# Recurrence with a mixture-of-experts layer: TensorE's up products three tiles ahead, VectorE's routing steps spread, scales of the sorted tiles on GpSimd, x and outputs in pairs of tiles

## The reference

```
h[t] = tanh(x[t] @ Wx + b + h[t-1] @ Wh)            # per batch element
shared  = silu(h @ w1_shared.T) @ w2_shared.T       # hidden width 1024
logits  = h @ gate_w.T                              # 8 experts
top 2 experts of each token, gates = softmax of the two logits
out = x + shared + sum over the token's 2 experts of gate * (silu(h @ w1_e.T) @ w2_e.T)
```

## Time and profile before

| | us |
|---|---|
| median of three runs | 382.14 |
| lowest, highest | 379.4, 389.73 |
| the profiled execution | 384.39 |
| its span | 382.6 |
| TensorE, ScalarE, VectorE, GpSimd busy | 357.1, 239.3, 197.2, 103.4 |
| mean granted TensorE clock, share of full speed | 0.985 |

### The profile page before, as it was taken

One profiled execution on the slowest core, in us unless ns is written; L12 is line 12 of the kernel. 1 busy time (PEld: TensorE's weight loads), 2 busy tenths in 40 slices (PEclk: granted clock), 3 DMA queues, 4 the chain that ended last, 5 costly groups with the idle time before them and its releaser, 6 DMA issues.

```text
span 382.6 us, 8882 instructions
## 1 busy us (share of the span) xinstructions
PE 357.1 (93%) x2440; PEld 252.5 (66%) x2441; DVE 197.2 (52%) x421; ACT 239.3 (63%) x462; POOL 103.4 (27%) x99
## 2 busy tenths in 40 slices
PE   7979999988897799899999999999999999999991
PEld 6758899954664465565666666666666666666670
DVE  0599999977999784574432333332333323233310
ACT  2877888875965675583566565666555666555630
POOL 1000001000027888220032522333322333322342
PEclk9999999999999699999999999999999999999997
DMA  7999999408699999698999898888888888888982
GB/s 222 430 428 433 422 398 334 147 17 134 153 177 230 229 265 223 175 210 172 193 155 135 158 165 145 161 153 153 152 148 144 159 152 153 151 150 144 160 138 29
DMA packets 167322, 75.55 MB, mean 197 GB/s; under 512 B 149504, under 2 KB 163968, under 8 KB 166016
## 3 DMA queue, kind: packets, MB, share of 16 engines
q1 hardware_dynamic: 155408, 61.93, 66.4%
q0 software_dynamic: 6864, 9.11, 15.8%
q10 hardware_dynamic: 5024, 4.20, 4.0%
HBM read 23.68 MB, written 16.53 MB: 105 GB/s over the span
## 4 chain that ended last, share of the span: by engine, by line
PE 73%; DMA 7%; SPq 6%; issue 5%; ACT 3%; another core or an unknown queue 2%; DVE 1%; POOL 1%; POOLq 0%; ACTq 0%
PE py L1170 28%; PE z L1062 27%; PE z L1078 8%; PE z L1043 4%; SPq L352 3%; PE z L1011 2%; SPq L378 2%; DMA space<-x_cols 2%; DMA space<-space 1%; DMA sorted_rows<-space 1%; PE px L1054 1%; ACT space L912 1%; PE py L1011 1%; DMA out<-space 1%
## 5 line engine op out<-in xcount | busy, mean ns | idle before, releaser
L1170 PE MATMUL py<-w_slots,space 128*128 (+1 forms) x1272 | 149.7, 274 | 7.0 <-DMA space<-recurrence_w 3.1
L1062 PE MATMUL z<-w_slots,x 128*128 (+1 forms) x636 | 148.4, 382 | 5.0 <-issue 4.1
L1170 PEld LDWEIGHTS py<-w_slots,space 128*128 128x128 f16 x1272 | 124.6, 98 | 35.5 <-issue 7.6
L1062 PEld LDWEIGHTS z<-w_slots,x 128*128 128x128 f16 x636 | 62.2, 98 | 71.8 <-issue 9.7
L912 ACT ACTIVATE space<-z,tile_scales 128x512 f32<-128x512 f32 x106 | 71.8, 677 | 50.6 <-PE z L1062 41.7
L488 POOL DMA_INDIRECT out<-space x37 | 58.2, 1574 | 153.2 <-issue 56.3
L637 DVE SCALAR_TENSOR_TENSOR recurrence_w<-space,tile_scales,recurrence_w 128x512 f16<-128x512 f32 x54 | 40.3, 751 | 75.8 <-ACT recurrence_w L919 64.8
L637 DVE SCALAR_TENSOR_TENSOR space<-space,tile_scales 128x512 f16<-128x512 f32 x52 | 38.7, 750 | 62.6 <-ACT space L919 53.4
L581 DVE SCALAR_TENSOR_TENSOR w_slots<-w_slots,w_scale 128x1024 f16<-128x1024 f32 x36 | 46.2, 1285 | 1.0
L919 ACT ACTIVATE recurrence_w<-space,tile_scales 128x512 f16<-128x512 f32 x54 | 39.0, 722 | 9.9 <-ACT space L912 3.1
L919 ACT ACTIVATE space<-space,tile_scales 128x512 f16<-128x512 f32 x52 | 37.5, 722 | 7.7 <-ACT space L912 2.7
(11 more groups left out here) (121 smaller groups left out, 162.5 us busy)
## 6 DMA issues: line engine op xcount, KB each, us to landing
w_slots<-weights SPq DMA_DIRECT2D x8, 2048.0 KB, 30.4
sorted_rows<-pad_row SPq DMA_DIRECT2D x1, 5070.0 KB, 57.7
w_slots<-weights SPq DMA_DIRECT2D x2, 1024.0 KB, 10.4
space<-x_rows ACTq DMA_DIRECT2D x16, 128.0 KB
out<-space ACTq DMA_DIRECT2D x16, 128.0 KB
space<-x_cols SPq DMA_DIRECT2D x3, 512.0 KB, 9.7
space<-recurrence_w SPq DMA_TRANSPOSE x55, 2.4
space<-space SPq DMA_TRANSPOSE x52
```

Of the source, the lines that this page charges most:

```text
L1062: last = nc.tensor.matmul(Z[u % 2][h][:], x16[:, u, x_part, k], weight(f, k * HID + h * BANK, BANK, part), start=k == 0 and x_part == 0 an ...
L1170: last = nc.tensor.matmul(PY[p][:, 0:D], hiddenT[:, p, low, q], weight(f, MATRIX + q * D, D, part), start=q == 0 and not low and part == 0 ...
```

## The change

It touches the shared stage and what prepares the sorted one.

- TensorE does the up products of tiles 2 and 3 before the down product of tile 0 and stays three tiles ahead (`LEAD`). The loop holds tiles 1 to 12; the down product of tile 13 follows alone. In this stage `up` waits for each half of `Z` by itself. `Z`, `PY` and the turned copies keep two buffers each.
- ScalarE takes the silu of tile 0's first half before it waits for the branch on `drift_known`. The code of the branch not taken is shorter, and one `If` on TensorE is two.
- VectorE: `states_low`, the halves of tiles 0 and 1 and the routing steps are interleaved; `route_gates` is after `route_choice`, `route_slots` at g = 2, `route_rows` at g = 3, the last `find_scales` at g = 6, `route_tiles` at g = 10; `shared_y(g - 3)` comes ahead of the side work; weight splits start at g = 4 instead of 3.
- The scales of the sorted tiles are made by GpSimd after its last scatter, with 12 instructions instead of VectorE's 6; the reduction of the last bounds comes after the first tile's scatters. ScalarE's first `high` no longer waits for `tiles_ok` but for `scales_ok`, at g = 7.
- SyncE: six row buffers instead of eight; one row transpose ahead of each part of tile 0's turn instead of three behind; other tables. The first two pairs of x are loaded in the recurrence. Later loads and the stores move two tiles in one DMA each.

```diff
-SORT_RING = 8
+SORT_RING = 6
+LEAD = 3
+PAIRS = TILES // 2
-ROWS_AT = {0: (0, 1, 2), 1: (3,), 3: (4, 5), 4: (6, 7), 5: (8, 9), **{t - 4: (t,) for t in range(10, TILES)}}
+ROWS_AT = {1: (2,), 2: (3, 4), 3: (5,), 4: (6,), 5: (7, 8), 6: (9, 10), 7: (11,), 8: (12, 13), 9: (14,), 10: (15,)}
...
+            sp.wait_ge(xproj_mm, K * BLOCKS)
+            for j in range(2):
+                sp.dma_start(x_res[:, 2 * j:2 * j + 2], x_pairs[j]).then_inc(x_res_in[j], 16)
...
             def turn_row(t):
                 sp.wait_ge(x_lo_ok, t + 1)
-                if t == RING:
-                    sp.wait_ge(routed, 1)
                 if t >= SORT_RING:
-                    sp.wait_ge(sorted_ok[t % SORT_RING], 16 * TOP)
+                    sp.wait_ge(sorted_ok[t % SORT_RING], 16 * TOP * (t // SORT_RING))
...
+            turn_first()
+            turn_row(0)
+            turn_part(0, 0, 0)
+            turn_row(1)
+            turn_part(0, 0, 1)
...
+            def make_scales():
+                def step(instruction):
+                    steps[0] += 1
+                    instruction.then_inc(table_step, 1)
+                    pool.wait_ge(table_step, steps[0])
+                steps = [0]
+                pool.wait_ge(experts_ok, 1)
+                pool.wait_ge(scales_ok, 1)
+                for n in range(3):
+                    step(nc.gpsimd.tensor_mul(scale_parts, is_expert,
+                                              ffn_scales[:, n, 1:FFNS].unsqueeze(1).broadcast_to([P, SLOT_TILES, E])))
+                    for half in (E // 2, E // 4):
+                        step(nc.gpsimd.tensor_add(scale_parts[:, :, 0:half], scale_parts[:, :, 0:half], scale_parts[:, :, half:2 * half]))
+                    step(nc.gpsimd.tensor_add(tile_scales[:, TILES:ALL_TILES, n], scale_parts[:, :, 0], scale_parts[:, :, 1]))
+                pool.sem_inc(tiles_ok, 1)
...
+                if t == 0:
+                    reduce_bounds(len(BOUND_BATCHES) - 1)
+                v = t - SORT_RING // 2
+                if 0 <= v < TILES - SORT_RING:
+                    waited(sorted_ok[v % SORT_RING], 16 * TOP * (v // SORT_RING + 1))
+                    nc.gpsimd.tensor_copy(hr[:, v % SORT_RING, D:ROW], meta[:, v + SORT_RING]).then_inc(row_copied, 1)
+            make_scales()
...
+            act.wait_ge(split_ok, 1)
+            act.wait_ge(up_mm, 1)
+            silu_first(hidden_ok)
             act.wait_ge(drift_known, 1)
...
+            def store(j):
+                v = j % 2
+                act.wait_ge(y_ok, 2 * j + 2)
+                nc.scalar.dma_start(out_pairs[j], ys[:, 2 * v:2 * v + 2]).then_inc(stored[v], 16)
+                if j + 2 < PAIRS:
+                    nc.scalar.dma_start(x_res[:, 2 * v:2 * v + 2], x_pairs[j + 2]).then_inc(x_res_in[v], 16)
...
-                if not (isinstance(g, int) and g < AHEAD):
-                    pe.wait_ge(hidden_ok, (g - 1) * HALVES)
                 for h in range(HALVES):
+                    if arrived is None:
+                        pe.wait_ge(hidden_ok, g * HALVES - (2 * HALVES - h - 1))
+                    elif h == 0:
+                        pe.wait_ge(hidden_ok, (g - 1) * HALVES)
                     up_half(u, f, h, up_mm)
...
             def shared(g, u, n):
-                up(g + AHEAD, (u + AHEAD) % RING, SHARED)
+                up(g + LEAD, (u + LEAD) % RING, SHARED)
                 down(g, u % 2, n, SHARED)
-            for g in range(2):
-                shared(g, g, 16 * (g // 2 + 1))
-            with pe.Fori(0, TILES // RING - 1) as i:
-                for u in range(2, 2 + RING):
+            up(AHEAD, AHEAD, SHARED)
+            shared(0, 0, 16)
+            with pe.Fori(0, (TILES - RING) // RING) as i:
+                for u in range(1, 1 + RING):
                     shared(i * RING + u, u, i * 32 + 16 * (u // 2 + 1))
+            down(TILES - LEAD, (TILES - LEAD) % 2, 16 * ((TILES - LEAD) // 2 + 1), SHARED)
```

More of the change, by code:

```diff
@@ L964, in _ @@
                     nc.scalar.mul(high, whole, scale).then_inc(high_ok, 1)
-                if g > AHEAD:
-                    store(g - AHEAD - 1)
+                if g >= LEAD + 2 and g % 2:
+                    store((g - LEAD - 2) // 2)
+            act.wait_ge(tiles_ok, 1)
             def expert(t, u, n, outs, indexed):
@@ L1124, in _ @@
                 pe.wait_ge(up_mm, 2 * HALVES)
+                pe.wait_ge(hidden_ok, 1)
                 with pe.Fori(0, GENERAL_ROUNDS) as r:
-                    inject_first()
                     pe.wait_ge(start_ok_general, r + 1)
-                    round_(z_mm_general, h_ok_general, r)
+                    for i in range(2):
+                        general_pair(r, i, i, first=i == 0)
+                    with pe.Fori(1, L // 4) as j:
+                        for p in range(2):
+                            general_pair(r, j * 2 + p, p)
+            with pe.If(same != EXPECTED_SAME):
                 for k in range(K):
```

191 lines of the change are left out of this document (100 added, 91 removed).

## The result

The changed kernel took 388.31 us in the median of four runs (387.0 to 389.3), the kernel before 381.11 us beside it (379.4 to 389.73). The ratio is 1.020, with a 95% interval of 1.014 to 1.026. I had forecast 375 us, 368 at the least and 382 at the most; it became slower, by an amount that lies on the 2% mark. The profiled execution of after took 387.0 us with a span of 385.3 us.

The account below looks back on a forecast made before the run. TensorE's products bound the sorted stage, so time could only come from some 15 us lost before it; 3.2 (start) + 1.3 (later wait) + 2.9 (slow matmuls) = 7.4 us off 382.14 gave 375 us, range 368 to 382.

Parts of the forecast that it names:

- Scales on GpSimd: Behind the last scatter: twelve GpSimd steps take 10.3 us, `tiles_ok` at 165.1 us; cost 0, bounds 0 and 3.7 us.
- the sum: Whole kernel: 3.2 + 1.3 + 2.9 = 7.4 us gained, taken off both the profiled execution and the median of 382.14 us.
- my slower rival: Before the sorted tiles: late last scatter and 1.24 us steps put `tiles_ok` at 180.7 us; 389 us, chance 0.07.
- Routing and sorting: Ahead of the sorted tiles: scatters begin sooner, last issued by 154.8 us, up product possible at 163.4 us; costs nothing.
- 2.6 us of cover: At the first sorted up product: sorted rows allow it at 163.4 us, below the 166.05 us at which TensorE gets there.
- Three tiles ahead: Start of the shared stage: the longer lead of up products removes 3.2 us of TensorE's waits, bounds 0.6 and 3.9.
- the 1.63, 0.78 and 0.76 us: Start of the shared stage: TensorE's waits for turned parts and VectorE's output of tile 0, all claimed to go.
- the 0.77 us that I had kept: Start of the shared stage: TensorE's wait for ScalarE's silu, claimed to stay because the branch behind stays.
- a rival (0.23): Shared stage: six row buffers and SyncE's queue turn all but the start's 3.2 us into waits; 379 us, chance 0.23.
- the next step: Later in the shared stage: the 1.30 us wait for tile 5's turned part goes; 0 if SyncE waits for scatters.
- Gaps of the trips: Up product 8 and the third trip's start: idle parts of 1.67 + 1.75 and 2.99 us claimed to stay.
- the slow part of 2.9 us: Behind the gaps in up product 8: matmuls slowed at the lower clock, claimed to go, 2.9 us, bounds 0 and 2.9.

Follow-up runs that it names:

- run 1: Changed kernel with the sorted tiles' scales back on VectorE, all else as changed: 379.6 us, ratio 1.004 to the kernel before.
- run 4: Changed kernel with one 128x4 copy more on GpSimd, behind the last scatter and ahead of the scales: 387.65 us in one execution.
- run 6: The kernel before, unchanged, measured and profiled a second time: 384.96 us, span 383.3 us.
- run 5: Kernel before with only the sorted tiles' scales moved to GpSimd behind the last scatter: 394.6 us in one execution, beside 382.9 us for before.
- run 8: Kernel before with 96 router instructions more in a branch never taken, so TensorE's shared-tile loop stands further on: 391.38 us, before 386.61 us, no verdict.
- run 11: Kernel before with only the up products three tiles ahead instead of two, shared outputs moved to match: 387.78 us, before 381.74 us, no ratio.
- run 12: Changed kernel with scales on VectorE and up products two tiles ahead again, outputs behind the routing steps: 385.58 us, ratio 1.013 to before.
- run 13: Changed kernel with scales on VectorE and row transposes 6 to 15 one or two places later on SyncE: 383.25 us, ratio 1.005 to before.
- run 14: Changed kernel with scales on VectorE and row transposes 6 to 15 each one place later on SyncE: 382.06 us, ratio 1.005 to before.
- run 15: Changed kernel with scales on VectorE and its two routing steps there moved sooner: 384.78 us, ratio 1.010 to before.
- run 16: Changed kernel with scales on VectorE, routing steps sooner, and the row transposes as in run 14: 383.51 us, ratio 1.007 to before.
- run 2: Changed kernel with one 128x4 sum more on GpSimd, ahead of its wait for the routing: 393.6 us in one execution.
- run 3: Changed kernel with one 128x4 sum more on GpSimd, between the scatters of tiles 12 and 13: 385.37 us in one execution.
- run 10: Kernel before with TensorE's loop over the shared tiles written out, nothing else: 382.48 us, ratio 1.010 to before.

## Why the prediction was wrong

Two steps of the prediction failed: the scales on GpSimd, which I put at a cost of 0, and the sum, whose 7.4 us did not come off the median. On the chip of run 1 the parts can be told apart. The kernel before took 378.02 us there; my forecast, 375/382.14 of it, would have been 371.0. Run 1 took 379.6, 8.6 us more, and run 4 with the scales on GpSimd 387.65, another 8.1 us. Of the 8.6 us, run 1's profile names 5.9 at down product 6 (4.25 of waiting and 4.46 - 2.78 = 1.7 of slow matmuls), for which my sum had no term; how the rest divides is not shown.

**Scales on GpSimd: the first step that failed.** I bounded twelve instructions by the durations of a VectorE product and of GpSimd's longest copy, and the busy time was inside the bounds: 6.6 us. What I left out is the gap that GpSimd takes to change from reductions to products, 8.38 us here, 5.9 to 8.4 us in every run that changed kinds. The last reduction across partitions stands at 109.69 us and the products behind the last scatter, so the gap falls on the path. `tiles_ok` came at 173.7 instead of 165.1 us. That is the threshold of my slower rival, 173.45 us, and about its result (389 us, at a chance of 0.07), but by another road: its steps of 1.24 us and its last scatter at 165.8 us were both wrong. And the price could be read. In the kernel before, GpSimd's timeline begins so:

```profile
1.23 0.32 POOL L423 MEMSET pad_row<- 128x260 f32 x1
9.18 0.28 POOL L425 TENSOR_SCALAR_AFFINE_SELECT identity<-identity 128x128 f32<-128x128 f32 x1 [7.63 <-issue]
```

That is 7.63 us ahead of the first instruction of a new kind, with nothing waited for, where it costs nothing. (The changed kernel no longer has this gap, as said above, but the trace I had in hand did.) I priced an absent operation by how long its neighbours run and did not ask what stands ahead of the first of a kind. The rule that I had from the Trainium skill, "GPSIMD Engine Reference", section "Engine selection", twice VectorE's time, was about the wrong term. Per instruction these products took 0.79 us against 0.48.

**Routing and sorting.** The first scatter, at 105.84 us, was in my range. The last was issued at 157.68 and done at 158.64 us, 52.8 us after the first; I had 47.8. So 32 scatters took 1.65 us each, not 1.5. GpSimd was busy for 38.4 us with them instead of 35.1; the bound reduction now stands between them (0.9 us), and 1.77 us were idle ahead of the last two. Why the scatters themselves ran longer is not shown. I called the gate at 163.4 us, with 3.5 us from the last landing to the up product, but in the kernel before TensorE did not wait there, so this was no price of the path. SyncE's request went out at 163.18, and in the runs that waited for it the product began 2.7 to 4.9 us after the request. So this path ends at 166 to 168 us, where my sum put TensorE. I counted on 2.6 us of cover; there was none. The request, on SyncE's timeline of the changed kernel:

```profile
163.18 2.50 SPq L374 DMA_TRANSPOSE x<-sorted_rows  x2
```

**Three tiles ahead.** At the start 3.94 us of waits fell to 0.91. That is 3.0 us where I said 3.2, but not by the same terms: of the 1.63, 0.78 and 0.76 us only 2.3 went, and the 0.77 us that I had kept went too. But the 3.0 us were not kept. Down product 6 gave back 4.58 us and about 2 us of slow matmuls: SyncE's wait for scatters behind six row buffers, which I had as a rival (0.23) and as the lower bound of the next step. Undoing it by SyncE's order only moved the loss to the sorted rows, and so did writing out the loop or taking the lead alone.

**Gaps of the trips.** Kept in the sum, and wrong. They are not a property of the place in the loop: in the changed kernel up products 8 and 12 begin without one. They vary from version to version and from run to run (in run 6 up product 8 has gaps of 0.79 and 0.37 us, not 1.67 and 1.75), and the slow part of 2.9 us that I dropped came back behind down product 6 (clock 0.72, as before).

**The sum: the second step that failed.** Its total agreed with run 1 (span 376.6 against 375.2), but that was luck, as the terms did not: what it lost at down product 6 it won at the trips' gaps. Against the medians it was worth nothing, ratio 1.004. I subtracted 7.4 us from an execution that was full of slow issue and took the same off the median. Beside run 1 the shortest executions of before took 376.63 us; no profile caught one of these, so what they hold is not shown.

**What stays open.** What makes TensorE issue single matmuls 0.7 us apart for 5 to 20 us. It was there in the three profiles of before and in runs 5, 8 and 11 to 16, and absent in runs 1 to 4, in both written-out loops, and in the changed kernel but for 0.5 us. The instruction packet does not explain it: in run 10 three more came inside this stretch, at 120.9, 145.0 and 160.3 us, without slow issue. That it is the jump back is only suggested by two profiles, and five others keep the loop and have none or next to none of it. The Trainium skill, in "Runtime: NRT & Kernel Launch", section "Instruction fetch mechanics", lets a taken branch outside the window pay for a fetch. By that rule the written-out versions should have been the faster ones. They were about 1% slower, and what made them so was not found beyond the wait for sorted rows in run 10. How much slow issue the short executions of before hold is open too.

## What to carry to other kernels

Before work moves to an engine, look in the trace for the first instruction of each kind on it and the idle time ahead: on GpSimd a change between reductions across partitions and elementwise products or sums cost 6 to 8 us each time, for 128x4 as for 128x312, and it must fall where the engine is idle anyway. Where two paths end within 2 us of each other (here TensorE's products and the scatters), taking waits out of one wins little; the sum has to be made for the second path to the same precision. And subtract a saving only from an execution whose stalls recur: profile the kernel before more than once, and take its shortest execution as the base of the forecast.

## What the runs showed of the hardware

- GpSimd's change of code: 7.29, 7.44, 8.16, 8.25, 8.38 and 7.22 us ahead of a two-operand product or sum, 5.93 us ahead of a reduction across partitions, 7.63 us ahead of an affine select in the kernel before and none in the changed one. Copies and scatters paid nothing on either side.
- On GpSimd a product of 128x312 took 0.78 to 0.88 us, a sum of 128x156 and one of 128x78 together 0.91 us, one of 128x39 0.26 us; on VectorE the product took 0.48 us.
- After 7.21 us of idleness TensorE's next 12 matmuls took 4.67 us instead of 2.75, in a stretch with a granted clock of 0.56; after 4.25 and 4.58 us, 24 took 4.46 and 4.88 instead of 2.78. After a wait of 2.60 us 12 took 4.45 (run 10), after one of 1.86 us 2.76 (run 11). After 2.63 us in run 16 24 took 2.79, so the last wait alone does not decide it.
- With its loop of twelve tiles written out, the same work in the same order, the kernel before took 1.0% longer (0.7 to 1.2%).
